# Sending the inner rows of eight shared tiles through DRAM, in one sequence with the experts' tiles

## The chip, the cores and the metric

The kernel runs on one core of a Trainium2 chip, as one program. The metric is the device time of one execution in microseconds (us). TensorE is called PE here, VectorE DVE, ScalarE ACT, GpSimd POOL and SyncE SP; each runs its own instructions strictly in order, and they wait for one another with semaphores. SP, ACT and POOL also issue DMAs, and a wait that stands ahead of a DMA in such a queue holds back all that stands behind it.

## The reference, cut to what matters

The first part (layer norm, attention over a context, gating) is not touched by the change. What follows it is a mixture of experts on 2048 tokens of 512 values, with 16 experts of inner width 352, four experts for each token, and two shared experts that every token passes:

```python
scores = jax.nn.softmax(xt @ Wg.T, axis=-1)
# two of four groups of experts are kept, and of these the best four experts: topi, weights
h = jax.nn.silu(jnp.einsum('td,eid->eti', xt, W1)) * jnp.einsum('td,eid->eti', xt, W3)
expert_out = jnp.einsum('eti,edi->etd', h, W2)
y = jnp.einsum('etd,te->td', expert_out, combine)
z = jax.nn.silu(xt @ Ws1.T) * (xt @ Ws3.T) @ Ws2.T
return (y + z).reshape(B, S, D)
```

The rows `h`, 352 values for each token, are called inner rows below: they are made by the two products with W1 and W3, and are the input of the product with W2.

## The kernel before

Tokens are worked in tiles of 128 rows. After attention there are three stages, in all 112 tiles: 16 tiles of the first shared expert (t = 0 to 15), 80 slots for the experts' tiles (E0 to E79 here; the last is never worked), and 16 tiles of the second shared expert. An expert's tile holds tokens of one expert, gathered by scattering each normed row four times into `xslot_d` in DRAM: POOL issues four indirect DMAs for each of the 16 token tiles (L626), out of a ring of four buffers `scat` that SP fills (L446).

Every fp32 operand of a product is split into a rounded part and a remainder (`xhi` and `xlo`, `hhi` and `hlo`, `whi` and `wlo`), and a product is three matmuls. So a tile goes through these steps:

- input rows: SP loads `xg` in four DMAs (L412), DVE transposes it into PSUM (L1492), ACT rounds it to `xhi` (L838), DVE takes the remainder `xlo` (L1499);
- `up` on PE: 24 matmuls of 352 columns (L1159 to L1161), twelve into a gate bank and twelve into bank 3;
- ACT takes silu of the gate bank into `sg` (L831), DVE multiplies with bank 3: the inner rows;
- the inner rows have to be turned, ACT rounds them to `hhi` (L877), DVE takes the remainder `hlo` (L1508);
- `down` on PE: nine matmuls of 512 columns (L1211 to L1213).

The stages differ in how inner rows are turned. In the first shared stage DVE writes `hx` (L1483), PE transposes it in three matmuls (L959, function `tr_h`), and the result is added to `x1` by DVE (L1561, called `res` in the rows). In the experts' stage DVE writes `hrow` (L1531), ACT stores it to `h_d` in DRAM in pieces of 96 values (L928, function `store_h`), SP loads it back as `hblk` (L468, `load_h`), and DVE turns 32x32 blocks (L1539, `h_turn`); there PE works the `up` of three later tiles between a tile's `up` and its `down`, which leaves the time for the way through DRAM, and the product is evacuated by ACT and stored.

While the first shared stage runs, ACT and DVE also split the second set of weights, in tiles 4 to 11 (L792 and L1448, two pieces for each tile), and DVE computes the routing tables in tiles 1 to 6.

The order of the instructions is set by two helpers. `pipeline` and `stream` write a stage as steps s; a part with a lead a works in step s on tile s + a, and the parts of a step stand in the order of the list. Before, the first shared stage is a `pipeline` on each engine, with the first experts' tiles added at its end by hand (`down_on`, `expert_high`, `expert_rows`, `first_row`), and the experts and the second shared stage are one `stream`. On PE a step of the first shared stage is `down` of tile s - 1, transposes of tile s, `up` of tile s + 1; a step of the experts is `down` of s - 2, `up` of s + 2. In the steps of SP, `load_scat` fetches the tile three ahead, and waits until the scatter of the tile before (s - 1) has left its buffer. Weights come in sets of 2.2 MB (`load_weights` and `next_raw` on POOL).

Of the kernel before, what the change touches and what calls it, by code (L numbers as in the profile page):

```python
# [14 lines left out]
P = 128  # L15
# [5 lines left out]
NQ = P // Q  # L21
# [24 lines left out]


# [48 lines left out]
def stream(eng, phases, ring, ramp=2):  # L96

    aheads = [a for ph in phases for a, fn in ph[2]]
    most, least = max(aheads), min(aheads)
    starts = [sum(ph[0] for ph in phases[:i]) for i in range(len(phases) + 1)]  # L100

    def peeled(s):
        for i in range(len(phases[0][2])):
            for p, (tiles, looped, parts, each_pass) in enumerate(phases):
                ahead, fn = parts[i]
                t = s + ahead - starts[p]
                if 0 <= t < tiles and fn:
                    fn(t, t % ring, t // ring)

    at = -max(0, most)  # L110
    for p, (tiles, looped, parts, each_pass) in enumerate(phases):
# [21 lines left out]
def xattn_moe(nc, x, heads, wg, wo, gn, wr, wexp, tables, qdecay, out):  # L133
    outer = ExitStack()
    with outer:
# [112 lines left out]
        sg = sb3("sg", [P, INTER], F32)  # L248
# [80 lines left out]
        def gate_bank(base, p):  # L329
            return 7 if base == NT and p else 2  # L330
# [19 lines left out]
        def _(sp):  # L350
# [82 lines left out]
            def store_y(t, r, turn):  # L433
                p = r % 2
                sp.wait_ge(y_out, 2 + NT + t + 1)
                sp.dma_start(rows(yslot_d, t), ysb[:, p, :]).then_inc(y_stored[p], 16)
# [6 lines left out]
            def load_scat(t, r, turn):  # L443
                if type(t) is not int or t >= XR:
# [16 lines left out]

            def load_h(t, r, turn):
                if type(t) is int and t == NR - 1:
                    return
                hold(sp, h_stored[r], 16 * (turn + 1))
                if type(t) is not int or t >= XG:
# [3 lines left out]
            sp.wait_ge(y_zeroed, 16 * (NR - NT * TOPK) // 8)  # L470
            stream(sp, [(NR, True, [(-1, load_h), (XG + 1, load_slots), (-3, store_y)], None),
                        (NT, False, [(0, None), (XG + 1, load_tile(NT + NR, xn_d)), (-4, store_out)], None)], XG)
# [191 lines left out]
        def _(act):  # L664
# [158 lines left out]
            def silu_g(base):  # L823
                def fn(t, p, half):
# [6 lines left out]
                    act.activation(sg[:, :], ps[:, gate_bank(base, p), 0:INTER], ACT.Silu).then_inc(silu, 1)  # L831
# [51 lines left out]
            def y_evac(t, p, half):  # L883
                act.wait_ge(mm2, NT + t + 1)
# [29 lines left out]
            def expert_high(t, p, half):  # L914
                if type(t) is int and t >= NT - 2:
                    x_high(NT)(t - NT + 2, p, 0)

            def x_high_e(t, p, half):
                if type(t) is not int or t >= 2:
                    x_high(NT)(t, p, half)  # L920

            def store_h(t, r, turn):
# [3 lines left out]
                if type(t) is not int or t >= XG:  # L926
                    hold(act, h_loaded[r], 16 * turn)
# [14 lines left out]
            pipeline(act, NT, [(1, x_high_on), (0, silu_on), (0, h_high(0)), (0, second_high), (0, exponents), (0, expert_high)], ramp=12)  # L942
            stream(act, [(NR, True, [(0, by_two(silu_g(NT))), (0, store_h), (-2, high_first), (2, by_two(x_high_e)), (-2, high_later), (-3, by_two(y_evac))], None),
                         (NT, True, [(0, by_two(silu_g(NT + NR))), (0, None), (-1, by_two(h_high(NT + NR))), (2, by_two(x_high(NT + NR))), (0, None), (0, None)], None)], XG)
# [3 lines left out]
        def _(pe):  # L948
# [184 lines left out]
            def up(base, which, halves=(0, 1)):  # L1133
                def fn(t, r, turn):
# [3 lines left out]
                    if base == NT:  # L1138
                        pe.wait_ge(silu, base + t - 1 if type(t) is not int or t else base)
# [94 lines left out]
            def routed(t, entry):  # L1234
                if type(t) is int:
# [15 lines left out]
            def down_on(t, r, turn):  # L1251
                if type(t) is int and t == NT - 1:
                    pe.wait_ge(rt_done, 1)
# [622 lines left out]
```

## Time and profile before

| what | us |
|---|---|
| median of 3 runs | 925.2 |
| lowest and highest run | 923.93 and 928.39 |
| profiled execution, its own time | 923.42 |
| span of the profiled execution | 921.8 |
| first shared stage, first `up` to the end of its last `down` | 235.8 to 350.5 |
| experts' stage after it, to the last `hblk` load | to 814.3 |

The profile is that of one execution. A row of the timeline gives the start in us from the start of the span, the duration, the engine, the line of kernel.py, the operation, and in brackets the idle time of the engine before it with what ended that. A row of windows gives the busy time of each engine in a stretch. The line of PE in 40 slices is nines almost throughout, and the granted clock (PEclk) is 9 in all of them.

### The profile page before, as it was taken

The numbers are of one execution on the slowest core, as the hardware profiler recorded it, in microseconds if no ns is written. First come the engines' busy times: TensorE is split into PE (matmuls) and PEld (weight loads), VectorE is DVE, ScalarE is ACT, GpSimd is POOL, SyncE is SP. The second block draws the span as 40 slices with busy tenths as digits, with TensorE's granted clock in tenths as the row PEclk, the third lists the DMA queues.
The fourth block names the chain that finished last, engine by engine and source line by source line (L and its number), as shares of the span: only waits on it lengthen the run. The fifth ranks groups of instructions, "written<-read, shape, count | busy, mean of one in ns | idle before, by whom it ended". The sixth has DMA issues, their size and how long they took to land.

```text
span 921.8 us, 19364 instructions
## 1 busy us (share of the span) xinstructions
PE 899.1 (98%) x4962; PEld 804.1 (87%) x4963; DVE 557.3 (60%) x1105; ACT 331.7 (36%) x708; POOL 494.5 (54%) x346
## 2 busy tenths in 40 slices
PE   8999998899989999999999999999999999999998
PEld 5778886688889999899999999999999999989997
DVE  6656676888896644544444444444444444459997
ACT  4556554354324322333333333333333333332221
POOL 1127777774167764435646664446666643136772
PEclk9999999999999999999999999999999999999999
DMA  6829996655578956778778777778777755588874
GB/s 216 267 100 393 384 404 232 225 187 175 189 232 296 306 208 206 230 204 253 238 240 246 251 247 202 239 244 259 249 251 250 245 173 158 163 228 248 274 247 145
DMA packets 180649, 218.97 MB, mean 238 GB/s; under 512 B 56576, under 2 KB 124160, under 8 KB 180224
## 3 DMA queue, kind: packets, MB, share of 16 engines
q1 hardware_dynamic: 118080, 123.49, 41.7%
q0 software_dynamic: 20816, 79.44, 25.9%
q10 hardware_dynamic: 41712, 15.54, 6.2%
q8 instruction: 20, 0.33, 0.2%
q14 instruction: 21, 0.17, 0.1%
HBM read 127.38 MB, written 91.03 MB: 237 GB/s over the span
## 4 chain that ended last, share of the span: by engine, by line
PE 78%; DVE 10%; issue 4%; ACT 3%; DMA 3%; ACTq 0%; DVEq 0%; POOL 0%; SPq 0%
PE ps L1159 15%; PE ps L1160 14%; PE ps L1161 14%; PE ps L1211 8%; PE ps L1213 8%; PE ps L1212 8%; PE ps L1012 2%; PE ps L1025 2%; DVE st L1456 1%; PE ps L959 1%; DVE res L1454 1%; DVE st L1273 1%; DMA hblk<-h_d 1%; ACT res L692 1%; PE ps L1045 1%
## 5 line engine op out<-in xcount | busy, mean ns | idle before, releaser
L1159 PE MATMUL ps<-whi,xhi 128*128 (+1 forms) x888 | 288.2, 325 | 1.6 <-issue 1.0
L1161 PE MATMUL ps<-whi,xlo 128*128 (+1 forms) x888 | 286.4, 323 | 0.0
L1160 PE MATMUL ps<-wlo,xhi 128*128 (+1 forms) x888 | 286.3, 322 | 0.0
L1531 DVE TENSOR_TENSOR hrow<-ps,sg 128x352 f32<-128x352 f32 x95 | 49.7, 524 | 214.4 <-ACT sg L831 211.1
L1159 PEld LDWEIGHTS ps<-whi,xhi 128*128 128x128 f32 x888 | 167.1, 188 | 6.5 <-issue 1.6
L1160 PEld LDWEIGHTS ps<-wlo,xhi 128*128 128x128 f32 x888 | 167.2, 188 | 3.9
L1161 PEld LDWEIGHTS ps<-whi,xlo 128*128 128x128 f32 x888 | 166.9, 188 | 0.0
L831 ACT ACTIVATE sg<-ps 128x352 f32<-128x352 f32 x111 | 51.5, 464 | 268.3 <-PE ps L1161 268.3
L838 ACT ACTIVATE xhi<-ps 128x512 fp32r<-128x512 f32 x112 | 66.9, 597 | 145.8 <-DVE ps L1492 145.8
L566 POOL TENSOR_TENSOR wlo<-raw,whi 128x2816 fp32r<-128x2816 f32 x16 | 100.7, 6293 | 2.4 <-POOL whi L564 0.2
L658 POOL DMA_INDIRECT raw<-yslot_d,sloti x64 | 68.1, 1064 | 57.7 <-DMA yslot_d<-ysb 22.6
L1499 DVE TENSOR_TENSOR xlo<-ps,xhi 128x512 fp32r<-128x512 f32 x112 | 76.9, 687 | 27.1 <-ACT xhi L838 26.8
L568 POOL CAST whi<-raw 128x1536 fp32r<-128x1536 f32 x16 | 23.5, 1468 | 126.2 <-PE ps L1213 126.2
L626 POOL DMA_INDIRECT xslot_d<-scat,sloti x64 | 62.8, 982 | 34.7 <-issue 17.7
L1492 DVE STREAM_TRANSPOSE ps<-xg 128x512 f32<-128x512 f32 x112 | 80.3, 717 | 0.0
L1211 PE MATMUL ps<-whi,hhi 128*128 (+1 forms) x168 | 67.3, 401 | 1.9 <-DVE hlo L1508 1.5
L1211 PE MATMUL ps<-whi,hhi_odd 128*128 (+1 forms) x165 | 65.2, 395 | 3.2 <-DVE hlo_odd L1508 3.2
L1213 PE MATMUL ps<-whi,hlo 128*128 (+1 forms) x168 | 66.6, 397 | 0.0
L1212 PE MATMUL ps<-wlo,hhi 128*128 (+1 forms) x168 | 66.2, 394 | 0.0
L1213 PE MATMUL ps<-whi,hlo_odd 128*128 (+1 forms) x165 | 65.0, 394 | 0.0
L1212 PE MATMUL ps<-wlo,hhi_odd 128*128 (+1 forms) x165 | 64.7, 392 | 0.0
L570 POOL TENSOR_TENSOR wlo<-raw,whi 128x1536 fp32r<-128x1536 f32 x16 | 56.3, 3518 | 2.3
(201 smaller groups left out, 1580.9 us busy)
## 6 DMA issues: line engine op xcount, KB each, us to landing
raw<-wexp_in POOLq DMA_DIRECT2D x18, 2176.0 KB, 11.4
xslot_d<-zero SPq DMA_DIRECT2D x10, 2048.0 KB, 21.7
xg<-xslot_d SPq DMA_DIRECT2D x320, 64.0 KB, 2.7
yslot_d<-ysb SPq DMA_DIRECT2D x80, 256.0 KB, 2.4
h_d<-hrow ACTq DMA_DIRECT2D x79, 192.0 KB, 2.9
hblk<-h_d SPq DMA_DIRECT2D x79, 192.0 KB, 2.6
xg<-xn_d SPq DMA_DIRECT2D x128, 64.0 KB, 3.6
xq<-x_in SPq DMA_DIRECT2D x16, 256.0 KB, 3.2
```

The source lines that it names most:

```text
L566: pool.tensor_tensor(wlo[:, p, up], raw[:, p, up], whi[:, p, up].bitcast(F32), ALU.subtract).then_inc(w13_ready, 1)
L626: pool.indirect_dma_start(out=xslot_d, out_offset=bass.IndirectOffsetOnAxis(ap=sloti[:, t * TOPK + k:t * TOPK + k + 1], axis=0), in_=scat[ ...
L658: pool.indirect_dma_start(out=gath[:, t % GR, k, :], out_offset=None, in_=yslot_d, in_offset=bass.IndirectOffsetOnAxis(ap=sloti[:, t * TOP ...
L838: act.activation(xhi[:, p, :], ps[:, p, :], ACT.Copy).then_inc(x_hi, 1)
L1159: pe.matmul(ps[:, bank, 0:INTER], xh, wh, start=(k == 0), stop=False)
L1160: pe.matmul(ps[:, bank, 0:INTER], xh, wl, start=False, stop=False)
L1161: mm = pe.matmul(ps[:, bank, 0:INTER], xl, wh, start=False, stop=(k == KT - 1))
L1211: pe.matmul(ps[:, 5 + p, :], hh, wh, start=(k == 0), stop=False)
L1212: pe.matmul(ps[:, 5 + p, :], hh, wl, start=False, stop=False)
L1213: mm = pe.matmul(ps[:, 5 + p, :], hl, wh, start=False, stop=(k == IC - 1))
L1492: dve.transpose(ps[:, p, :], xg[:, r, :].rearrange("p (c k j) -> p k c j", c=NQ, k=KT)).then_inc(x_tr, 1)
L1499: dve.tensor_tensor(xlo[:, p, :], ps[:, p, :], xhi[:, p, :].bitcast(F32), ALU.subtract).then_inc(x_lo, 1)
```

## The change

1. The first eight shared tiles stay as they were, but for one thing: DVE writes `hx` in an order that is already turned in blocks, since the shared expert's W2 rows are now stored in that order for all of its 16 tiles. That takes two instructions instead of one (`h_mult`).
2. The last eight shared tiles are now tiles -8 to -1 of the experts' sequence. Their inner rows go through DRAM like an expert's, they use gate banks 7 and 2 in turn instead of bank 2 alone, and PE transposes nothing for them. `add_later` adds their products to `x1`.
3. `stream` takes for each phase where it starts and its first tile, and all engines run one stream of three phases. In a step in which two phases meet, input rows' rounding (`x_high`) and remainder (`x_low`) stand ahead of the additions and of the inner rows' rounding and remainder.
4. On PE the last eight tiles are brought up two steps ahead: the order around the seam is up 7, up 8, down 6, transposes 7, up 9, down 7, up 10, up 11, down 8, up 12. The seam between shared tiles and experts, with its own hand-written order, is gone.
5. On SP the loads of inner rows stand in the same queue as the fetches for the scatter (`scat_later`, now four tiles ahead instead of three), and the first experts' rows are loaded at fixed steps (`load_rows`).

```diff
+HT = NT // 2
+HR = HT // XG
...
-            return 7 if base == NT and p else 2
+            return 7 if base == NT and p == 0 else 2
...
-            pipeline(sp, NT, [(XG, next_tile), (3, load_scat)], ring=XG)
-            sp.wait_ge(zeroed, 16 * (NR // 8))
-            sp.wait_ge(rt_done, 1)
...
+            def scat_later(t, r, turn):
+                if type(t) is int and t < 0:
+                    load_scat(t + NT, r, turn + NT // XG)
...
-            stream(sp, [(NR, True, [(-1, load_h), (XG + 1, load_slots), (-3, store_y)], None),
-                        (NT, False, [(0, None), (XG + 1, load_tile(NT + NR, xn_d)), (-4, store_out)], None)], XG)
+            stream(sp, [(0, 0, HT, False, [(0, None), (XG, next_tile), (0, None), (3, load_scat)], None),
+                        (NT, -HT, NR, True, [(-1, load_h), (XG + 1, load_rows), (-3, store_y), (XG, scat_later)], None),
+                        (NT + NR, 0, NT, False, [(0, None), (XG + 1, load_tile(NT + NR, xn_d)), (-4, store_out), (0, None)], None)], XG)
...
-            pipeline(pe, NT, [(-1, down_on), (0, tr_h(0)), (1, up_on)], ring=XG, ramp=3)
-            stream(pe, [(NR, True, [(0, None), (-2, down(NT, routed)), (2, up_e)], load_words),
+            stream(pe, [(0, 0, HT, False, [(-1, down(0, first)), (0, tr_h(0)), (1, up_on)], None),
+                        (NT, -HT, NR, True, [(0, None), (-2, down(NT, routed)), (2, up(NT, routed))], load_words),
...
-                    dve.tensor_tensor(hx[:, 0:INTER], ps[:, 3, 0:INTER], sg[:, :], ALU.mult).then_inc(h_ready, 1)
+                    up_half = ps[:, 3, 0:IC * P].rearrange("p (c k j) -> p c k j", c=NQ, k=IC)
+                    gates = sg[:, :].rearrange("p (c k j) -> p c k j", c=NQ, k=IC)
+                    turned = hx[:, :].rearrange("p (k c j) -> p c k j", k=IC, c=NQ)
+                    dve.tensor_tensor(turned[:, :, 0:2, :], up_half[:, :, 0:2, :], gates[:, :, 0:2, :], ALU.mult)
+                    dve.tensor_tensor(turned[:, 0:3, 2:3, :], up_half[:, 0:3, 2:3, :], gates[:, 0:3, 2:3, :], ALU.mult).then_inc(h_ready, 1)
...
+            stream(dve, [(0, 0, HT, False, [(2, x_turn_on), (1, x_low_on), (0, h_mult_on), (0, route_1), (0, route_2), (0, None), (-1, add_shared(0)),
+                                            (0, h_low_on), (0, second_set), (0, None)], None),
+                         (NT, -HT, NR, True, [(0, h_row(NT)), (-2, turn_first), (-2, low_first), (2, x_turn(NT)), (-2, turn_later), (2, x_low(NT)), (-2, low_later),
+                                              (-3, add_later), (0, second_later), (0, None)], None),
```

**On PE, where tiles 7 and 8 meet.** Before, `up` of a shared tile stands behind a `down` (here tile 7's, ending with L1213) and the three transposes of the next tile:

```order
L1213 MATMUL ps<-whi,hlo_odd 128x512
L1221 REGISTER_ALU
L959 MATMUL ps<-const,hx 128x128 [waits h_lo,h_ready]
L959 MATMUL ps<-const,hx 128x128 x2
L1137 REGISTER_ALU
L1159 MATMUL ps<-whi,xhi 128x352 [waits w13_ready,h_ready,x_lo]
```

In the changed kernel the last matmuls of tile 7's `up` are followed by the first of tile 8's:

```order
L1188 MATMUL ps<-wlo,xhi 128x352
L1189 MATMUL ps<-whi,xlo 128x352
L1187 MATMUL ps<-whi,xhi 128x352 [waits rt_done,w13_ready,silu,x_lo]
L1188 MATMUL ps<-wlo,xhi 128x352
L1189 MATMUL ps<-whi,xlo 128x352
```

No `down` and no transposes stand between the two, and tile 8's `up` waits for the routing tables (`rt_done`) and for an earlier silu.

**On DVE, tiles 7 and 8.** Before: input rows of the tiles ahead (L1492, L1499), the inner rows (`hx`), the addition of the tile before (`res`), the remainder `hlo`, two pieces of the second weights (`wlo`):

```order
L1492 STREAM_TRANSPOSE ps<-xg 128x512
L1499 TENSOR_TENSOR xlo<-ps,xhi 128x512
L1483 TENSOR_TENSOR hx<-ps,sg 128x352
L1561 TENSOR_TENSOR res<-res,ps 128x512
L1508 TENSOR_TENSOR hlo_odd<-ps,hhi_odd 128x384
L1448 TENSOR_TENSOR wlo<-raw,whi 128x272 x2
L1492 STREAM_TRANSPOSE ps<-xg 128x512
L1499 TENSOR_TENSOR xlo<-ps,xhi 128x512
L1483 TENSOR_TENSOR hx<-ps,sg 128x352
```

In the changed kernel, from the inner rows of tile 7 to those of tile 8 (`hrow`) and the next input rows:

```order
L1506 TENSOR_TENSOR hx<-ps,sg 128x4x2x32
L1507 TENSOR_TENSOR hx<-ps,sg 128x96
L1516 STREAM_TRANSPOSE ps<-xg 128x512
L1523 TENSOR_TENSOR xlo<-ps,xhi 128x512
L1585 TENSOR_TENSOR res<-res,ps 128x512
L1532 TENSOR_TENSOR hlo_odd<-ps,hhi_odd 128x384
L1468 TENSOR_TENSOR wlo<-raw,whi 128x272 x2
L1555 TENSOR_TENSOR hrow<-ps,sg 128x352
L1516 STREAM_TRANSPOSE ps<-xg 128x512
L1523 TENSOR_TENSOR xlo<-ps,xhi 128x512
```

The product is now two instructions, input rows moved behind it, and the inner rows of tile 8 stand behind the addition and the remainder that belong to tiles 6 and 7.

**On SP, at the end of the fetches for the scatter.** Before, the last fetch is followed by the first experts' rows (`xslot_d`), and the first load of inner rows comes only after six of these:

```order
L446 DMA scat<-xn_d 128x512 [waits scattered2]
L85 REGISTER_ALU
L85 COMPARE_AND_BRANCH
L446 DMA scat<-xn_d 128x512 [waits scattered3]
L454 TENSOR_LOAD order [waits y_zeroed,rt_done,zeroed]
L454 ISA x2
L412 DMA xg<-xslot_d 32x4x128 [waits scattered0,c_loaded,scattered1,scattered2,x_tr,scattered3]
L412 DMA xg<-xslot_d 32x4x128 x3
```

In the changed kernel, from the load of input rows of tile 13 to the load of inner rows of tile 9:

```order
L415 DMA xg<-xn_d 32x4x128 [waits x_tr]
L415 DMA xg<-xn_d 32x4x128 x3
L453 DMA scat<-xn_d 128x512 [waits scattered0]
L493 DMA hblk<-h_d 128x384 [waits h_stored0,c_loaded]
L415 DMA xg<-xn_d 32x4x128 [waits x_tr]
L415 DMA xg<-xn_d 32x4x128 x3
L453 DMA scat<-xn_d 128x512 [waits scattered1]
L493 DMA hblk<-h_d 128x384 [waits h_stored1,c_loaded]
```

A load of inner rows stands behind each fetch that waits for a scatter.

## Rows read from the trace of the kernel before

**Rows 1.** The page, busy us, share of the span, instructions:

```profile
PE 899.1 (98%) x4962; PEld 804.1 (87%) x4963; DVE 557.3 (60%) x1105; ACT 331.7 (36%) x708; POOL 494.5 (54%) x346
```

**Rows 2.** Timeline of PE, shared tiles (first two), then experts' (others); start, duration:

```profile
300.44 0.49 PE L959 MATMUL ps<-const,hx 128*128 128x128 f32 x3
306.70 0.49 PE L959 MATMUL ps<-const,hx 128*128 128x128 f32 x3
...
561.39 0.32 PE L1159 MATMUL ps<-whi,xhi 128*128 x1
567.32 0.32 PE L1159 MATMUL ps<-whi,xhi 128*128 x1
```

**Rows 3.** Timeline of PE around the `up` of shared tile 7:

```profile
288.20 0.41 PE L1159 MATMUL ps<-whi,xhi 128*128 128x352 f32 x1
...
292.12 0.39 PE L1211 MATMUL ps<-whi,hhi 128*128 128x512 f32 x1
...
294.20 0.49 PE L959 MATMUL ps<-const,hx 128*128 128x128 f32 x3
294.45 0.41 PE L1159 MATMUL ps<-whi,xhi 128*128 128x352 f32 x1
```

**Rows 4.** Timeline of DVE after the transposes of tile 8:

```profile
301.49 0.56 DVE L1508 TENSOR_TENSOR hlo<-ps,hhi 128x384 fp32r<-128x384 f32 x1 [0.17 <-ACT hhi L877]
301.96 0.78 DVE L1448 TENSOR_TENSOR wlo<-raw,whi 128x272 fp32r<-128x272 f32 x2
302.67 0.72 DVE L1492 STREAM_TRANSPOSE ps<-xg 128x512 f32<-128x512 f32 x1
```

**Rows 5.** SP's queue: two fetches for the scatter, then waits from 256 to 345 us:

```profile
307.17 0.35 SPq L446 DMA_DIRECT2D scat<-xn_d  x1
...
312.29 0.35 SPq L446 DMA_DIRECT2D scat<-xn_d  x1
...
SPq L446 <- DMA xslot_d<-scat,sloti: 42.9, 12, 15.8
```

**Rows 6.** DMAs to landing: L928, L468; then `xg` at 270:330 and 420:600:

```profile
DMA to landing us min/median/max: 2.1/2.9/11.4
...
DMA to landing us min/median/max: 2.1/2.6/9.9
...
xg<-xn_d SPq DMA_DIRECT2D x36, 64.0 KB, 3.5
...
xg<-xslot_d SPq DMA_DIRECT2D x125, 64.0 KB, 2.4
```

**Rows 7.** Timeline at the first experts' tiles: POOL's weight load, DVE, PE:

```profile
356.39 0.96 POOL L480 DMA_DIRECT2D raw<-wexp_in  x1
...
367.09 0.59 DVE L1539 STREAM_TRANSPOSE ps<-hblk 128x384 f32<-128x384 f32 x1 [3.31 <-DMA hblk<-h_d]
...
369.01 0.50 PE L1211 MATMUL ps<-whi,hhi_odd 128*128 x1 [0.83 <-DVE hlo_odd L1508]
```

**Rows 8.** Timeline of PE, tiles 1 and 3, then of DVE in tiles 0 and 1:

```profile
258.82 0.50 PE L1211 MATMUL ps<-whi,hhi_odd 128*128 128x512 f32 x1 [0.88 <-DVE hlo_odd L1508]
...
273.04 0.50 PE L1211 MATMUL ps<-whi,hhi_odd 128*128 128x512 f32 x1 [1.46 <-DVE hlo_odd L1508]
...
243.21 0.29 DVE L1586 TENSOR_TENSOR gcmp<-gcmp,const 128x128 f32<-128x128 f32 x1
...
251.55 0.53 DVE L1483 TENSOR_TENSOR hx<-ps,sg 128x352 f32<-128x352 f32 x1 [1.02 <-ACT sg L831]
252.00 0.16 DVE L1613 COPY ntile<-ps 128x16 f32<-128x16 f32 x1
252.19 0.43 DVE L1614 TENSOR_TENSOR tcmp<-ntile,const 128x256 f32<-128x256 f32 x1
```

**Rows 9.** Windows: busy us of PE, PEld, DVE, ACT, POOL; clock, DMA share, GB/s:

```profile
306.00:312.00 6.00, 6.00 (x36) 5.61 (x35) 3.60 (x7) 2.08 (x5) 4.47 (x6) 1.00 0.92 310
312.00:318.00 6.00, 6.00 (x36) 5.63 (x35) 3.44 (x8) 2.08 (x5) 4.53 (x5) 1.00 0.97 328
390.00:410.00 20.00, 19.77 (x112) 18.35 (x112) 9.73 (x17) 6.88 (x14) 7.13 (x3) 1.00 0.74 224
```

**Rows 10.** DMA queue of the stores of inner rows, 420 to 600 us: packets, MB, share:

```profile
q10 hardware_dynamic: 16374, 6.10, 12.5%
```

**Rows 11.** POOL's last scatter; the scatters' issues at 270:330 with us to landing:

```profile
340.14 0.97 POOL L626 DMA_INDIRECT xslot_d<-scat,sloti  x1 [0.30 <-issue]
...
xslot_d<-scat,sloti POOLq DMA_INDIRECT x47, 4.0
```

More of the change, by code:

```diff
@@ L96, in stream @@
 def stream(eng, phases, ring, ramp=2):
-    aheads = [a for ph in phases for a, fn in ph[2]]
+    aheads = [a for ph in phases for a, fn in ph[4]]
     most, least = max(aheads), min(aheads)
-    starts = [sum(ph[0] for ph in phases[:i]) for i in range(len(phases) + 1)]
+    starts = [ph[0] for ph in phases] + [phases[-1][0] + phases[-1][2]]
     def peeled(s):
-        for i in range(len(phases[0][2])):
-            for p, (tiles, looped, parts, each_pass) in enumerate(phases):
+        for i in range(len(phases[0][4])):
+            for p, (start, first, tiles, looped, parts, each_pass) in enumerate(phases):
                 ahead, fn = parts[i]
-                t = s + ahead - starts[p]
-                if 0 <= t < tiles and fn:
+                t = s + ahead - start
+                if first <= t < tiles and fn:
                     fn(t, t % ring, t // ring)
     at = -max(0, most)
-    for p, (tiles, looped, parts, each_pass) in enumerate(phases):
+    for p, (start, first, tiles, looped, parts, each_pass) in enumerate(phases):
         lo = starts[p] + min(max(0, ramp - least), tiles)
@@ L460, in load_slots, with load_rows @@
                 load_tile(NT, xslot_d)(t, r, turn)
+            def load_rows(t, r, turn):
+                if type(t) is not int or t > 5:
+                    load_slots(t, r, turn)
+                elif t < 0:
+                    load_tile(0, xn_d)(t + NT, r, turn)
+                elif t == 0:
+                    sp.wait_ge(zeroed, 16 * (NR // 8))
+                    sp.wait_ge(rt_done, 1)
+                    load_slots(0, 0, 0)
+                elif t == 1:
+                    load_slots(1, 1, 0)
+                elif t == 4:
+                    load_slots(2, 2, 0)
+                    load_slots(3, 3, 0)
+                elif t == 5:
+                    load_slots(4, 0, 1)
+                    load_slots(5, 1, 1)
+            def scat_later(t, r, turn):
+                if type(t) is int and t < 0:
+                    load_scat(t + NT, r, turn + NT // XG)
             def load_h(t, r, turn):
@@ L912, in exponents, with second_later @@
                     act.activation(top8f[:, :, 0:TOPK], top8f[:, :, 0:TOPK], ACT.Exp).then_inc(rt_exp, 1)
[L914 to L920, printed above, removed]
+            def second_later(t, p, half):
+                if type(t) is int and t < 0:
+                    second_high(t + NT, p, half)
             def store_h(t, r, turn):
@@ L1138, in fn @@
                     if base == NT:
-                        pe.wait_ge(silu, base + t - 1 if type(t) is not int or t else base)
+                        pe.wait_ge(silu, base + t - 1)
+                        if type(t) is int and t == -HT:
+                            pe.wait_ge(rt_done, 1)
                     elif 1 in halves:
@@ L1234, in routed @@
             def routed(t, entry):
+                if type(t) is int and t < 0:
+                    return 0, 1
                 if type(t) is int:
```

83 lines of the change are left out of this document (34 added, 49 removed).

## The prediction

> **What bounds the kernel now.** I read the page first: PE is busy for 98% of the span [rows 1]. So only two things can move the time by much: less work on PE, or a new stall of PE. Then the timeline of PE, a shared tile against an expert's. From transposes to transposes a shared tile takes 306.70 - 300.44 = 6.26 us, an expert's tile from `up` to `up` 567.32 - 561.39 = 5.93 us [rows 2]. The pieces: `up` with its slow first matmul 292.12 - 288.20 = 3.92 us, `down` 294.20 - 292.12 = 2.08 us, transposes 0.25 us [rows 3]; an expert's `up` is then 5.93 - 2.08 = 3.85 us. The difference of 0.33 us is what a PE transpose of inner rows costs a tile. Last, the stalls: PE waits for DVE by 0.88 us in tile 1 and 1.46 us in tile 3, where the routing tables delay `hlo` [rows 8], and by 0.83 us at the second expert's tile, whose inner rows came late from DRAM behind a weight load [rows 7].
>
> **The change part by part.** (a) Eight tiles lose their transposes: 8 x 0.33 = 2.64 us less on PE, which nothing else can hide. The granted clock is full at every stretch I looked at (1.00 in [rows 9]), so no gain or loss comes from there.
>
> (b) The old seam to the experts goes. It cost PE 0.83 us: the load of the second tile's rows sat in flight while 2.2 MB of weights, issued at 356.39, were moving [rows 7]. In the new order the experts come in mid-stream, with three `up`s between a tile's `up` and its `down`. The weights still come, some 5 us later, since POOL splits the shared W2 only after tile 15's `down`, which is now behind two experts' `up`s. What such a load costs mid-stream is read from a 20 us window around one: PE busy 19.77 us, 0.23 us lost [rows 9]. I take 0.83 - 0.23 = 0.60 us gained, between 0 and 0.83.
>
> (c) `h_mult` is two instructions. One of 352 columns lasts 0.53 us and the next starts 0.45 us after it; 256 columns start the next 0.46 us later, with 0.43 us of their own; 128 columns last 0.29 us [rows 8]. Two pieces of 256 and 96 so cost between 0.1 and 0.3 us more; I take 0.13, since issue overlaps the tail of an instruction by some 0.08 us. It matters only where DVE is late already: tiles 0, 1 and 3 with the routing tables, and tile 6, four times: 0.5 us, from 0.4 to 1.2. In the other tiles the product ends about 0.85 us before PE reaches the transposes.
> The Trainium skill (VectorE: DVE Perf Modes, The TRN2 errata) gives an fp32 `tensor_tensor` (N + 151)/0.96 ns, so a second instruction would add 0.16 us; by that the term would be 0.63 us, an estimate. The trace agrees for 256 columns (0.43 us [rows 8], 0.42 by the page).
>
> (d) The new seam. I go along PE from the old clock, where tile 7's `up` ends at 292.12 [rows 3]. Up 8 to 295.97 (3.85 us), down 6 to 298.05, transposes to 298.30, the gate half of up 9 (half of 3.92 us) to 300.2. Its second half overwrites bank 3 and waits for the row product of tile 8. On DVE that product now stands behind the addition of tile 6, which waits for down 6; behind `hlo` of tile 7, which in the old rows starts 1.05 us after the transposes do (301.49 - 300.44) [rows 2, 4]; and behind two pieces of weights, 0.71 us (302.67 - 301.96) [rows 4]. So: 298.05 + 1.05 = 299.1, + 0.47 + 0.71 = 300.3, + 0.53 for the product: 300.8. PE waits 0.6 us, between 0 (if the pieces overlap better) and 0.9 (two more signals).
>
> (e) Inner rows of tile 8. Their store is issued at 301.3. SP loads them only behind the fetch for the scatter in its queue, which in the old trace comes free at 307.17 [rows 5]; POOL sets this pace and nothing of POOL changes. Load issued at 307.6. A landing takes 2.6 us in the median, but here the DMA engines are 92 to 97% taken [rows 9], and `xg` loads take 3.5 us where they take 2.4 among the experts [rows 6]: 2.6 x 3.5/2.4 = 3.8 us, 311.4. From the turn on DVE to the first matmul of `down` are 369.01 - 367.09 = 1.92 us [rows 7]: 313.3. PE wants it after up 9 (302.8), down 7, up 10 and up 11: 302.8 + 2.08 + 2 x 3.85 = 312.6. It waits 0.7 us. Bounds: with the fastest landing of a load, 2.1 us, 0; with the slowest, 9.9 us [rows 6], 6.8. I take 0.7, by the `xg` loads of the same stretch.
> Tile 9: load at 312.29 + 0.4, ready at 312.7 + 3.8 + 1.92 = 318.4; PE wants it at 313.3 + 2.08 + 3.85 = 319.2. Each later tile gains 5.93 - 5.12 = 0.8 us on the fetches (312.29 - 307.17 [rows 5]). Nothing more is lost there.
>
> (f) First experts' rows. The last scatter is issued at 340.14 and lands by 340.14 + 0.97 + 4.0 = 345.1 [rows 11]. SP then issues four loads, about 2 us, landing in 2.4, and transpose, rounding and remainder take 2 us: E2 is ready at 351.4. PE, at 319.2 + 4 x 5.93 = 342.9 after E0's `up`, comes to E2's after down 13, up E1, down 14: 342.9 + 2 x 2.08 + 3.85 = 350.9. 0.5 us late; 0 if POOL, which waited for PE before its last two tiles, ends sooner.
>
> SP's other waits, POOL's indirect DMAs and ACT's extra stores cost nothing themselves: ACT is busy 2.08 of 6 us there, DVE 3.6 of 6 [rows 9], and DVE gets about 0.5 us of turning more for each tile.
>
> The sum: -2.64 - 0.60 + 0.5 + 0.6 + 0.7 + 0.5 = -0.94 us. The profiled execution took 923.42 us, so 922.5 for one like it; it lies 1.8 us under the median of the three runs, 925.2, and I take the same difference there: 924.3 us. A change of 0.5% is 4.6 us, about what a measurement of this kernel can tell from no change.
>
> **The rivals.** *All covers hold.* DVE's order costs nothing at up 9, the load of tile 8 lands in 2.1 us, the scatter ends in time: -2.64 - 0.83 + 0.4 = -3.1, or 922.1 us. For it speaks the 60% of DVE [rows 1]; against it that SP cannot issue tile 8's load before 307.6.
>
> *The DMA engines are over-full: slower.* The stretch of scatters is at 92 to 97% [rows 9]. A store of inner rows takes 12.5% x 180 us / 30 = 0.75 us of all engines [rows 10], in the 180 us and 30 stores of that window, and the load back about as much again: of 5.93 us, 25%. If shares add, demand is 1.19 of what there is, and the scatters of a tile take 6.1 us instead of 5.12. Over eight tiles that is 7.8 us, less some 1.7 us that POOL waited for PE at the end: about 6 us, and E2's rows are that much later, one for one. That gives -0.94 + 6 = +5.1: 930.3 us. It turns the change into a loss from 0.9 us of slip, and into one over 0.5% from 5.5 us. Against it: `xg` loads in this stretch still land in 3.5 us [rows 6], which engines at their limit would not give, and the share is busy time of packets, not of bandwidth (328 GB/s there [rows 9]).
> The Trainium skill (DMA: Bandwidth & Descriptors, Specifications) wants at least 512 B for each transfer, below which an engine reads, modifies and writes; it speaks against this change, whose stores go in pieces of 96 values. The trace agrees that these stores are dear: 6.10 MB in 16374 packets take 12.5% [rows 10]. By that rule alone it is this rival, and 930.3 us.
>
> *The transposes were hidden.* PE's records are modelled at their ends, and if the 0.33 us were waiting for the product and not work, taking the transposes away gives nothing: 925.2 - 0.94 + 2.64 = 926.9. Against it: 0.25 us pass between the start of the transposes and the next `up`, with no wait shown [rows 3].
>
> **How the numbers follow.** Forecast (a sum near -0.9, from -2.5 to +2): 0.60, at 924.3. All covers hold: 0.20. Over-full engines: 0.13. Hidden transposes: 0.05. Anything else 0.02. The range runs from 921.5 (all covers, and a little of the runs' own spread) to 930.5 (the over-full engines at their price); beyond it are the higher half of that rival, and half of the rest. Faster by over 0.5% needs a gain of 4.6 us, more than (a) and (b) hold: 0.03. Slower by over 0.5%: 0.10. Within: 0.87.
>
> **What would show it.** In the changed kernel's trace: no PE transposes after tile 7, and 5.93 us for each shared tile from tile 12 on; PE waits of 0.6 us in the second half of tile 9's `up`, 0.7 us at tile 8's `down`, 0.5 us at E2's `up`, none at the second expert's `down`; SP's fetches for the scatter still 5.1 us apart. Wrong: fetches 6 us apart, PE waiting for `hblk` in more than one tile, or PE's waits in tiles 1 and 3 longer by more than 0.3 us each.

## The result and the profile after

The changed kernel takes 928.44 us (median of 20 runs, 925.34 to 930.73), the kernel before 923.82 us (median of 20 runs, 921.52 to 928.39). The ratio is 1.0047, its 95% interval 1.0036 to 1.0057: slower, by 4.6 us. The forecast was no change that can be measured, at 924.3 us; the time lies inside the range given, and on the other side of no change from the sum, which was a gain of 0.94 us. The profiled execution took 928.44 us, its span is 926.8 us.

On the page of the changed kernel PE is about as full as before [rows 1] (97% of the span, 98% before), with fewer instructions and more busy time:

```profile
PE 903.5 (97%) x4938; PEld 806.3 (87%) x4939; DVE 561.9 (61%) x1121; ACT 333.1 (36%) x708; POOL 493.8 (53%) x346
```

So matmuls became longer or further apart somewhere. To find where, I compared the two timelines of PE at points with equal work behind them: the first matmul of the second product (`down`) of every 128-row tile, counted in the order of work (the sixteen shared tiles, then E0, E1 and so on).

| stretch, first matmul of a `down` to first matmul of a later one | before | after | difference |
|---|---|---|---|
| shared tile 0 to expert tile E2 (the seam lies in it) | 124.91 | 125.97 | +1.06 |
| E2 to E8 | 36.07 | 36.62 | +0.55 |
| E8 to E74 (66 tiles, no stall in either trace) | 390.06 | 392.92 | +2.86 |
| E74 to tile 13 of the second shared stage | 110.08 | 110.47 | +0.39 |
| sum | 661.12 | 665.98 | +4.86 |

The first stretch has the seam that the prediction spoke of; the third, the largest difference, has nothing that it spoke of. The third is also the firmest: as shown below, kernels with the same buffer layout repeat its time to the hundredth, while the first stretch takes 123.5 to 125.5 us in twelve single executions that work it with the instructions of before.

**The seam.** The timeline of PE in the changed kernel, the rows with a wait and one of the matmuls that follow the longest (start, duration, then the wait in brackets):

```profile
301.09 0.43 PE L1187 MATMUL ps<-whi,xhi 128*128 128x352 f32 x1 [0.39 <-DVE hrow L1555]
...
315.52 0.50 PE L1239 MATMUL ps<-whi,hhi 128*128 128x512 f32 x1 [2.15 <-DVE hlo L1532]
...
316.94 0.63 PE L1240 MATMUL ps<-wlo,hhi 128*128 128x512 f32 x1
...
319.07 0.50 PE L1187 MATMUL ps<-whi,xhi 128*128 128x352 f32 x1
...
401.19 0.49 PE L1239 MATMUL ps<-whi,hhi 128*128 x1 [0.63 <-DVE hlo L1532]
```

Tile 9's `up` waits 0.39 us for the row product, tile 8's `down` 2.15 us for its remainder. That `down` then takes 319.07 - 315.52 = 3.55 us where one took 2.08 [rows 3]: its matmuls last 0.63 us instead of 0.39. The windows of the changed kernel say why (busy us of PE, PEld, DVE, ACT, POOL; clock, DMA share, GB/s):

```profile
310.00:330.00 20.00, 17.85 (x93) 16.22 (x92) 11.61 (x22) 5.82 (x13) 15.37 (x16) 0.91 1.02 347
...
316.20:319.00 2.80, 2.80 (x8) 2.19 (x7) 2.24 (x5) 1.52 (x4) 2.19 (x3) 0.50 1.05 385
```

The granted clock is 0.50 from 316.2 to 319.0, the lower of the two levels (1.2 GHz); where the same stretch had been at 1.00 before [rows 9]. The chain back from the wait is on DVE and in SP's queue:

```profile
313.76 0.59 DVE L1563 STREAM_TRANSPOSE ps<-hblk 128x384 f32<-128x384 f32 x1 [3.24 <-DMA hblk<-h_d]
```

```profile
301.91 0.34 SPq L453 DMA_DIRECT2D scat<-xn_d  x1
302.30 4.33 SPq L415 DMA_DIRECT2D xg<-xn_d  x4
309.04 0.34 SPq L453 DMA_DIRECT2D scat<-xn_d  x1
309.47 0.38 SPq L493 DMA_DIRECT2D hblk<-h_d  x1
```

The load of tile 8's inner rows (L493) goes out at 309.47, right behind a fetch for the scatter that waited for its buffer until 309.04, and lands 4.3 us later.

**The experts.** An even step runs from the first matmul of an even tile's `down` (input `hhi`) to that of the next tile's (`hhi_odd`), an odd step from there to the next `hhi`. The timeline of PE in the changed kernel, first matmuls of three successive `down`s, and in each of the two `up`s between them three matmuls of its second half:

```profile
562.08 0.39 PE L1239 MATMUL ps<-whi,hhi_odd 128*128 x1
...
566.72 0.32 PE L1188 MATMUL ps<-wlo,xhi 128*128 x1
566.88 0.32 PE L1189 MATMUL ps<-whi,xlo 128*128 x1
567.04 0.32 PE L1187 MATMUL ps<-whi,xhi 128*128 x1
...
567.99 0.39 PE L1239 MATMUL ps<-whi,hhi 128*128 x1
...
572.49 0.33 PE L1187 MATMUL ps<-whi,xhi 128*128 x1
572.66 0.33 PE L1188 MATMUL ps<-wlo,xhi 128*128 x1
572.82 0.33 PE L1189 MATMUL ps<-whi,xlo 128*128 x1
...
573.98 0.39 PE L1239 MATMUL ps<-whi,hhi_odd 128*128 x1
```

From `hhi_odd` to `hhi` a step takes 5.91 us, from `hhi` to `hhi_odd` 5.99 us. The difference is in the second half of the `up` of even tiles, where matmuls start 0.166 us apart and not 0.16. No wait is shown and the clock is 1.00. An even step of the kernel before, with three matmuls of the same place:

```profile
565.23 0.39 PE L1211 MATMUL ps<-whi,hhi 128*128 x1
...
569.73 0.32 PE L1159 MATMUL ps<-whi,xhi 128*128 x1
569.89 0.32 PE L1160 MATMUL ps<-wlo,xhi 128*128 x1
570.04 0.32 PE L1161 MATMUL ps<-whi,xlo 128*128 x1
...
571.15 0.39 PE L1211 MATMUL ps<-whi,hhi_odd 128*128 x1
```

It takes 5.92 us, with these starts 0.15 to 0.16 us apart. Over E8 to E74 the even steps average 6.00 us and the odd ones 5.91; before, 5.92 and 5.90. 33 pairs of tiles times 11.907 - 11.820 are the 2.86 us of the table.

### The profile page after: what moved, and what is told of

The parts are those of the page before. It is cut to its first block, busy times and chain, and to the rows that moved or that the text cites. A ratio compares the mean times of both kernels' runs of the same rounds, so it can differ in the third digit from the quotient of the medians.

```text
span 926.8 us, 19226 instructions
## 1 busy us (share of the span) xinstructions
PE 903.5 (97%) x4938; PEld 806.3 (87%) x4939; DVE 561.9 (61%) x1121; ACT 333.1 (36%) x708; POOL 493.8 (53%) x346
## 4 chain that ended last, share of the span: by engine, by line
PE 74%; DVE 8%; issue 7%; DMA 5%; ACT 3%; POOL 3%; ACTq 0%; DVEq 0%; SPq 0%; POOLq 0%
PE ps L1187 14%; PE ps L1189 13%; PE ps L1188 13%; PE ps L1239 8%; PE ps L1241 8%; PE ps L1240 7%; POOL xslot_d L651 3%; DMA xslot_d<-scat,sloti 2%; PE ps L1038 2%; PE ps L1051 2%; DMA h_d<-hrow 1%; DVE st L1476 1%; DVE res L1474 1%; DVE st L1293 1%; ACT res L717 1%
## 5 line engine op out<-in xcount | busy, mean ns | idle before, releaser
L1555 DVE TENSOR_TENSOR hrow<-ps,sg 128x352 f32<-128x352 f32 x103 | 53.9, 523 | 223.3 <-ACT sg L856 219.4
```

## Experiments

Steps named even and odd below are means over these 33 pairs. Single executions of these kernels differ by up to 4 us in stretches that an edit doesn't touch, so where only one execution was made, the verdict rests on the steps and not on the time. The ratios are those on record; they differ a little from the quotients of the two medians (1.0005 and 1.0016 for e3), which all lie inside the intervals given.

**What slows the even tiles.** Two lines of the change could reach into the experts' loop, whose instructions are otherwise the same: the order of the gate banks, and the size of the buffer `sg`, which the diff ahead of the prediction leaves out (`sb3("sg", [P, INTER], F32)` became `[P, IC * P]`, for the view in `h_mult`). Each was put into the kernel before, alone; neither adds an instruction, so the place where the loop's instructions lie, a third possible cause, stays as it was.

```diff
-            return 7 if base == NT and p else 2
+            return 7 if base == NT and p == 0 else 2
```

> The kernel before with one line changed: among the experts the first product of the even tiles goes to PSUM bank 7 and that of the odd ones to bank 2, as in the changed kernel (before: odd to 7, even to 2). In the changed kernel an even tile's step takes 6.00 us and an odd one's 5.91; before 5.92 and 5.90. Theory A, the bank order makes the even tiles' second half slow: steps 6.00 and 5.91 here too, 33 pairs times 0.085, +2.9 us, about 926.7. Theory B, the addresses in SBUF that move with the larger gate buffer, and theory C, where the loop's instructions lie: 5.92 and 5.90, no change beyond 0.5 us.

e1: 924.57 us against 924.73, ratio 0.9993 (0.9970 to 1.0015); steps 5.92 and 5.90. The banks do nothing.

```diff
-        sg = sb3("sg", [P, INTER], F32)
+        sg = sb3("sg", [P, IC * P], F32)
...
-                    act.activation(sg[:, :], ps[:, gate_bank(base, p), 0:INTER], ACT.Silu).then_inc(silu, 1)
+                    act.activation(sg[:, 0:INTER], ps[:, gate_bank(base, p), 0:INTER], ACT.Silu).then_inc(silu, 1)
...
```

(The two products of DVE read `sg[:, 0:INTER]` in the same way.)

> The kernel before with the gate buffer as large as the changed kernel has it (384 instead of 352 numbers a row, so that everything allocated behind it lies 128 bytes further on; nothing else is changed). Theory B (addresses): even steps 6.00, odd 5.91, about +2.9 us. Theories A (banks) and C (place of the instructions): 5.92 and 5.90, within 0.5 us of before.

e2: 928.89 us against 924.73, ratio 1.0037 (1.0013 to 1.0061). The timeline of PE, first matmuls of two successive `down`s:

```profile
566.59 0.39 PE L1211 MATMUL ps<-whi,hhi 128*128 x1
...
572.58 0.39 PE L1211 MATMUL ps<-whi,hhi_odd 128*128 x1
```

5.99 us, as in the changed kernel; E8 to E74 takes 392.92 us, to the hundredth what it takes there. A buffer that is 128 bytes longer, and whose extra bytes nothing here reads, makes the kernel before slower by 0.4%. The reverse in the changed kernel, first by the banks alone (shared tile 7 goes to bank 7, so that tile 8 finds bank 2 free), then by the addresses alone (the longer buffer is laid over the small table behind it):

```diff
-            return 7 if base == NT and p == 0 else 2
+            return 7 if base == NT and p or base == 0 and type(t) is int and t == HT - 1 else 2
...
```

> The changed kernel with the bank order of before among the experts (odd tiles to bank 7, even to bank 2; tile 7 of the shared expert goes to bank 7 so that tile 8 finds bank 2 free). Theory A: all steps 5.90 to 5.92 and 2.9 us less, about 925.5. Theories B and C: even steps stay at 6.00 and the time within 0.5 us of 928.4. The wait of 2.15 us at tile 8 stays in all.

e4: 928.87 us, ratio to before 1.0032 (1.0015 to 1.0050); steps 6.00 and 5.91.

```diff
-        sg = sb3("sg", [P, IC * P], F32)
-        ntile = sb3("ntile", [P, 2, E], F32)
+        sgn = sb3("sgn", [P, INTER + 2 * E], F32)
+        sg, ntile = sgn[:, 0:IC * P], sgn[:, INTER:INTER + 2 * E].rearrange("p (a e) -> p a e", a=2)
```

> The changed kernel with the gate buffer at its larger size laid over the small table that follows it, whose numbers are not read through it, so that every other buffer has the address it has in the kernel before; nothing else is changed. Theory (addresses): even steps among the experts back from 6.00 to 5.91 us, 2.9 us less, about 925.6. Rival, the larger gate buffer itself and not what it moves: even steps stay at 6.00, within 0.5 us of the changed kernel. The wait of 2.15 us at tile 8's second product stays in both.

e5: 924.64 us, ratio to before 1.0003 (0.9987 to 1.0020), and the steps are back:

```profile
566.40 0.39 PE L1239 MATMUL ps<-whi,hhi 128*128 x1
...
572.32 0.39 PE L1239 MATMUL ps<-whi,hhi_odd 128*128 x1
```

5.92 us, 390.06 us from E8 to E74. So addresses alone turn this change from the same into slower.

**Which buffer.** The kernel before again, with 128 unused bytes a row put ahead of one buffer, so that all behind it move. One execution each.

```diff
+        sb3("pad", [P, IC * P - INTER], F32)
         hrow = sb3("hrow", [P, 2, IC * P], F32)
```

> The kernel before with 128 unused bytes a row ahead of the inner rows' buffer hrow, so that only hrow and hblk move. If one of the two sets the even tiles' pace: even steps 6.00, odd 5.91. If it is hhi_odd and hlo_odd, or one of the buffers ahead of them (tables, ysb, scat): 5.92 and 5.90.

e7: 5.92 and 5.90 (928.16 us; the time went elsewhere, 3.9 us of it at the start of the second shared stage).

```diff
+        sb3("pad", [P, IC * P - INTER], F32)
         hhi.append(sb3("hhi_odd", [P, IC * P], F32R))
```

> The kernel before with 128 unused bytes a row ahead of hhi_odd, so that hhi_odd, hlo_odd (the weights that TensorE loads for the odd tiles' second product), hrow and hblk move. If these weights' addresses set the pace: even steps 6.00 and odd 5.91 here and 5.92 and 5.90 with the pad ahead of hrow. If it is ysb, scat or the tables: 5.92 and 5.90 in both.

e8: 6.00 and 5.91 (926.74 us). So it is `hhi_odd` and `hlo_odd`, the rows that TensorE loads as weights for the odd tiles' `down`. The same pad between the two, then pads of twice and three times the size ahead of both:

> The kernel before with the 128 unused bytes between hhi_odd and hlo_odd, so that hlo_odd moves and hhi_odd stays (hrow and hblk move too; the pad ahead of hrow showed that they do nothing). If the slow second halves of the even tiles' up come from hlo_odd: even steps 6.00 as with the pad ahead of hhi_odd. If from hhi_odd: 5.92. If each has its share: between, near 5.96.

e9: 5.92 and 5.94 (927.62 us). The even steps stay, as if `hhi_odd` set them; but the odd tiles' `down` itself, which reads these rows, takes 2.10 us instead of 2.06, which none of the three theories had. (In the changed kernel it takes 2.09, and the `up` behind it gives 0.02 back.)

> The kernel before with 256 unused bytes ahead of hhi_odd instead of 128. If it is the place within 256 bytes that counts (before 160, in the changed kernel 32): 160 again, even steps 5.92. If any move of the two buffers away from where they lay does it: 6.00.

> The kernel before with 384 unused bytes ahead of hhi_odd. If the place within 256 bytes counts, it is 32 as in the changed kernel: even steps 6.00. If only the changed kernel's own addresses are slow: 5.92.

e10, with 256 bytes: 5.92 and 5.90 (922.18 us). e11, with 384 bytes: 6.00 and 5.91 (924.95 us). Timeline of PE, even steps of the first, then of the second:

```profile
564.29 0.39 PE L1212 MATMUL ps<-whi,hhi 128*128 x1
...
570.21 0.39 PE L1212 MATMUL ps<-whi,hhi_odd 128*128 x1
```

```profile
565.31 0.39 PE L1212 MATMUL ps<-whi,hhi 128*128 x1
...
571.31 0.39 PE L1212 MATMUL ps<-whi,hhi_odd 128*128 x1
```

Moves by 0 and 256 bytes give 5.92, by 128 and 384 bytes 6.00: in these four, what counts is the place within 256 bytes, not where the buffers lie. Four more layouts asked for the rule: `hhi_odd` alone moved; `hhi` and `hlo` alone; both pairs by the same 128 bytes; the odd pair by 64.

> The kernel before with 128 unused bytes ahead of hhi_odd and 128 ahead of hlo_odd: hhi_odd lies at 32 within 256 bytes as in the changed kernel, hlo_odd, hrow and hblk at 160 as before. If hhi_odd alone sets the slow second halves: even steps 6.00. If it takes both: 5.92, perhaps with a longer odd step as in the run in which hlo_odd alone had moved (5.94).

> The kernel before with 128 unused bytes ahead of hhi and 128 behind the gate buffer: hhi and hlo (the even tiles' pair) lie at 224 within 256 bytes instead of 96, and everything behind the gate buffer lies at 256 more, the same place within 256. If the rule holds for every such pair: the odd tiles' up, which stands ahead of the product with hhi, takes some 0.08 us more or less, odd steps near 5.98 or 5.82. If it is one of the odd pair alone: 5.92 and 5.90 as before.

> The kernel before with 128 unused bytes ahead of hhi, so that hhi, hlo, the gate buffer and all behind it lie 128 further on: within 256 bytes hhi 224, hhi_odd 32, both at places that were slow when one pair alone had moved, but their distance is 64 as before. If the distance counts: even steps 5.92. If either place counts: 6.00.

> The kernel before with 64 unused bytes ahead of hhi_odd: the distance of the pairs is 128 within 256 bytes instead of 64. No theory gives a number for this distance: 5.92 if only 192 is slow, 6.00 or between if 64 is the one good distance seen so far.

e13 to e16, one execution each, took 928.73, 927.76, 928.46 and 927.55 us. All layouts side by side. The places are counted from the buffers' sizes in the order in which they are allocated; the traces hold no addresses, so what is certain is how far each buffer moved against before. The last column is the 33 pairs of E8 to E74 against before:

| runs | place of `hhi`, `hlo` within 256 B | of `hhi_odd`, `hlo_odd` | even step | odd step | us more |
|---|---|---|---|---|---|
| before, banks (e1), addresses back (e5), `hrow` (e7), 256 B (e10), two instructions (e12) | 96, 96 | 160, 160 | 5.92 | 5.90 | 0 |
| after, longer `sg` (e2), later fetch (e3), banks back (e4), 128 B (e8), 384 B (e11) | 96, 96 | 32, 32 | 6.00 | 5.91 | 2.86 |
| `hhi_odd` alone (e13) | 96, 96 | 32, 160 | 6.00 | 5.90 | 2.42 |
| `hlo_odd` alone (e9) | 96, 96 | 160, 32 | 5.92 | 5.94 | 1.32 |
| even pair moved (e14) | 224, 224 | 160, 160 | 5.98 | 5.91 | 2.20 |
| both moved by 128 B (e15) | 224, 224 | 32, 32 | 5.98 | 5.91 | 2.20 |
| odd pair by 64 B (e16) | 96, 96 | 224, 224 | 5.92 | 5.96 | 2.20 |

In the slow rows one second half of the two in a pair of tiles takes 1.98 us instead of 1.90 (in none of the first row, and none of e9's): that of the even tiles' `up`, but in the last row that of the odd tiles'. With `hhi` and `hlo` where they were, the place of `hhi_odd` goes with it. But moving the even pair does it too, in the same place of the step, and the distance between the pairs is not it either: 64 bytes in the first row and in the sixth, and the sixth is slow. (With the even pair the gate buffer moved as well, and in the sixth layout all that lies behind it; these were not moved alone.) A rule is not found. What is shown is that the layout of before is the best of seven, and that the pace follows the layout: the kernels of the first row take 390.06 us from E8 to E74, each of them, and those of the second 392.92 (e6 below, with the layout of the first row, 390.14). Why matmuls that read neither buffer start later stays open.

**The seam.** Is the load of tile 8's inner rows late because of its place in SP's queue, or because the DMA engines are full? The fetch was put one step later, so that the load stands behind one that has waited for less:

```diff
-                        (NT, -HT, NR, True, [(-1, load_h), (XG + 1, load_rows), (-3, store_y), (XG, scat_later)], None),
+                        (NT, -HT, NR, True, [(-1, load_h), (XG + 1, load_rows), (-3, store_y), (3, scat_later)], None),
```

> The changed kernel, but from tile 8 on the fetch for the scatter stands 3 tiles ahead on SP instead of 4, so that the load of tile 8's inner rows stands behind a fetch that waited for less. Theory: the 2.15 us wait at tile 8's second product comes from that queue order, and the 1.4 us of half clock behind it from the wait; both go, 3.5 us less, about 924.9 (span 923.3), clock 1.00 in 310 to 330. Rival, the load is late because the DMA engines are full (share 1.02 there): the wait stays within 0.5 us of 2.15 and the time within 1 us of 928.4. The even steps stay at 6.00.

e3: 926.24 us, ratio to before 1.0005 (0.9980 to 1.0029), 2.6 us less than the kernel with the banks put back, which has the wait and ran on the same chip. The wait at tile 8 is gone, and the even steps stay at 6.00. SP's queue, windows (columns as above) and PE in this kernel:

```profile
303.96 0.34 SPq L453 DMA_DIRECT2D scat<-xn_d  x1
306.34 0.34 SPq L493 DMA_DIRECT2D hblk<-h_d  x1
```

```profile
310.00:330.00 20.00, 19.42 (x109) 17.84 (x109) 13.07 (x26) 7.01 (x17) 15.42 (x16) 1.00 1.03 341
```

```profile
321.67 0.50 PE L1239 MATMUL ps<-whi,hhi_odd 128*128 128x512 f32 x1 [0.58 <-DVE hlo_odd L1532]
```

The engines are as full (1.03), so their share alone does not make the wait; with the other order, counted from tile 0's `down` in each trace, the load goes out 4.9 us earlier. What is left is 0.58 us at tile 9. The clock stays at 1.00. That the wait alone does not settle the clock is shown by the kernel with the banks put back: it waited 2.27 us at the same place and ran on at full clock, so the seam cost it 1.4 us less (124.59 us from tile 0 to E2, where the changed kernel took 125.97). PE and windows of that kernel:

```profile
316.00 0.50 PE L1239 MATMUL ps<-whi,hhi 128*128 128x512 f32 x1 [2.27 <-DVE hlo L1532]
316.34 0.39 PE L1240 MATMUL ps<-wlo,hhi 128*128 128x512 f32 x1
```

```profile
316.10:318.00 1.90, 1.90 (x9) 1.52 (x10) 1.23 (x3) 1.38 (x4) 1.29 (x3) 1.00 0.96 351
```

And by the kernel with the addresses put back, whose wait of 2.17 us was again followed by half clock:

```profile
316.60:319.90 3.30, 3.30 (x8) 2.62 (x9) 2.32 (x5) 1.59 (x4) 2.43 (x3) 0.50 1.04 384
```

Of three profiled executions with this wait, two lost the clock behind it. The Trainium skill (TensorE: Matmul & The Clock Gate, Part 1: The HAM clock gate) says that an idle engine falls to 1.2 GHz and gets 2.4 GHz back when it is busy; these two executions agree, with 0.50; the third, with the same wait, kept 1.00, and no run here shows what told them apart. Nor does the length of a wait tell it elsewhere: behind one of 1.89 us (E2, at 376.43) e16 was at 0.50, behind one of 3.38 us (at 849.49) e7 stayed at 1.00.

**Both.** The two edits that gave something, together:

> The changed kernel with both edits, the addresses of before and the fetch for the scatter 3 tiles ahead. If the two costs are separate: 2.5 us (what the later fetch gave) and 2.9 us less than the changed kernel, 923.0, some 1 to 2 us below the kernel before on the same chip. Rival, they overlap (one of them hides the other): 925 or more.

e6: 922.19 us against 924.28, ratio 0.9972 (0.9956 to 0.9988): 2.4 us less than with the addresses alone, and below both kernels. The two costs are separate. From tile 0 to E2 it takes 121.77 us, 3.14 less than before (whose own stretch is good to about 1 us, as said); 0.93 of that is given back by E8, where a store of inner rows issued at 380.00, beside a weight load issued at 379.21, lands 12.7 us later. Windows, then PE:

```profile
310.00:330.00 20.00, 20.00 (x115) 18.84 (x114) 13.23 (x25) 6.19 (x15) 15.16 (x16) 1.00 1.01 345
```

```profile
397.63 0.50 PE L1239 MATMUL ps<-whi,hhi 128*128 x1 [0.97 <-DVE hlo L1532]
```

**The product in two instructions.** The kernel before with this alone, at its own addresses (left out of the cut: the three views as in the change, the gate buffer laid over the small table as in e5, and the shared expert's W2 rows in the turned order):

```diff
-                    dve.tensor_tensor(hx[:, 0:INTER], ps[:, 3, 0:INTER], sg[:, :], ALU.mult).then_inc(h_ready, 1)
+                    dve.tensor_tensor(turned[:, :, 0:2, :], up_half[:, :, 0:2, :], gates[:, :, 0:2, :], ALU.mult)
+                    dve.tensor_tensor(turned[:, 0:3, 2:3, :], up_half[:, 0:3, 2:3, :], gates[:, 0:3, 2:3, :], ALU.mult).then_inc(h_ready, 1)
...
```

> The kernel before with the shared tiles' product written in two instructions in the turned order (and the rows of the shared expert's second weights in that order), at the addresses of before; all sixteen tiles still go through the transposes. The prediction had 0.13 us for each of the four tiles whose second product waits, 0.5 us in all. By the changed kernel's trace it is 0.20 us up to tile 5. Here: 0.2 us up to tile 5 and none from tile 8 on, if the waits are those of tiles 1 and 3 alone; 0.13 for each tile, 2 us by tile 15, if the product is on every tile's path.

e12: 924.55 us in one execution. Against before, the `down`s of tiles 1, 3 and 6 each start 0.06 to 0.07 us later, 0.20 in all by tile 7, and nothing is added up to tile 14. On DVE, in the changed kernel:

```profile
251.53 0.42 DVE L1506 TENSOR_TENSOR hx<-ps,sg 128x256 f32<-128x256 f32 x1 [1.02 <-ACT sg L856]
251.87 0.25 DVE L1507 TENSOR_TENSOR hx<-ps,sg 128x96 f32<-128x96 f32 x1
252.03 0.16 DVE L1637 COPY ntile<-ps 128x16 f32<-128x16 f32 x1
```

The next instruction starts 0.50 us after the product, where it was 0.45 [rows 8].

## Why the prediction was wrong, step by step

**(a) The transposes, -2.64 us: right in size.** At the addresses of before (e5) the shared tiles from 9 on take 5.90 and 5.92 us (forecast 5.93). The rival that they were hidden is out. In the changed kernel itself the slow even steps take back some 0.30 us of it by E2 (tile 9 to E2 takes 53.49 us, 53.19 in e5).

**"The granted clock is full at every stretch I looked at (1.00 in [rows 9]), so no gain or loss comes from there": failed.** The rows were right for a PE that never stops. Behind a wait of 2.15 us the clock was at 0.50, and `down` 8 took 1.5 us more. A wait that the change adds must be priced with what the clock does after it.

**(b) The old seam, -0.60 us: more, by the wrong subtraction.** The stall of 0.83 us is gone, and with it a second one at the next expert's tile that the rows ahead of the prediction leave out (375.50 below). The weight load that stood behind them goes out at 366.21 in the changed kernel, in mid-stream, and PE has no wait from 315.52 to 401.19. So it costs nothing there. The 0.23 us that I took for it belongs to the next set of weights (399.63 below), which both kernels load: issued at 382.25 before and at 383.32 now, where it shows as the 0.63 us at 401.19. In e4 and e5 PE doesn't wait there. PE in the kernel before:

```profile
375.50 0.49 PE L1211 MATMUL ps<-whi,hhi 128*128 x1 [0.23 <-issue]
...
399.63 0.50 PE L1211 MATMUL ps<-whi,hhi 128*128 x1 [0.23 <-issue]
```

What the old seam costs also differs by execution: in thirteen executions that have it, from E0 to E2 takes 12.4 to 14.0 us (13.47 in the trace before), so 0.83 is one value of several.

**(c) The product in two instructions, +0.5 us: too high.** 0.20 us, shown by itself in one execution (0.1 to 0.3 in the five with the change, by tile 5). The second instruction starts under the tail of the first: 0.05 us from start to start, not 0.13, and three tiles instead of four.

**(d) Tile 9's second half, +0.6 us: right mechanism,** 0.39 us.

**(e) Tile 8's inner rows, +0.7 us: right mechanism, wrong size.** 2.15 us, and 1.5 us of half clock behind it. The failed sub-step is "POOL sets this pace and nothing of POOL changes": the fetch came free at 309.04 and not at 307.17 [rows 5]. The same 1.9 us, counted from tile 0's `down`, are in the two other executions with this queue order. POOL did keep its pace; the landing of its scatter did not. The last indirect DMA of the scatter that this fetch waited for, before and in the changed kernel (its row on POOL, then the row of DMAs issued in that instant, with us to landing):

```profile
302.75 0.97 POOL L626 DMA_INDIRECT xslot_d<-scat,sloti  x1 [0.30 <-issue]
...
xslot_d<-scat,sloti POOLq DMA_INDIRECT x1, 4.4
```

```profile
302.67 0.97 POOL L651 DMA_INDIRECT xslot_d<-scat,sloti  x1 [0.30 <-issue]
...
xslot_d<-scat,sloti POOLq DMA_INDIRECT x1, 6.3
```

With the banks put back it takes 6.4 us too, with the later fetch (e3, e6) 4.8. So slower landings, as the rival of the over-full engines has them, have a part in this wait beside the order. The first store of inner rows, issued at 301.13, and a fetch issued at 301.91 that takes 5.4 us to land (3.2 before) are in flight with it; which of them slows it was not tried. The landing of the load itself took 4.3 us for 3.8. I had kept 6.8 as the upper bound and put no chance on what lies between.

**(f) E2's rows, +0.5 us: nothing.** No wait there. The sum was wrong too: a landing is counted from the start of the issue, so the 0.97 us stand in it twice (and its terms add up to 351.5, not 351.4). Counted once, the rows are ready at 350.5, ahead of PE's 350.9.

**The over-full engines: half of a rival.** DMAs in the changed kernel, 270 to 330 us, with us to landing in the last column, have the fetches at 4.1, the inner rows at 4.9:

```profile
scat<-xn_d SPq DMA_DIRECT2D x11, 256.0 KB, 4.1
...
hblk<-h_d SPq DMA_DIRECT2D x5, 192.0 KB, 4.9
xslot_d<-scat,sloti POOLq DMA_INDIRECT x47, 4.2
```

The engines' share is 1.02 from 310 to 330 us (0.88 before), and the fetches are 5.7 us apart from 296.42 to 324.85, not 5.1. One scatter that landed 1.9 us later made most of the wait under (e). But in the median the scatters land in 4.2 us (4.0 before [rows 11]), and no expert's rows were late. Its time, 930.3, was nearer than the forecast, for another reason; that 928.44 lies inside the range is luck, since this rival alone had set the upper end.

**What was not in the sum: the addresses, +2.9 us.** This is the step whose absence decided the sign: with the addresses put back and the late load still there, the change measures 1.0003 (0.9987 to 1.0020). The parts were priced from the instructions that the change adds and removes. A line that changes only a buffer's size has none, and was not among them.

With what was measured, from tile 0 to E2: -2.64 + 0.30 - 0.83 - 0.23 + 0.20 + 0.39 + 2.15 + 1.5 = +0.84, where the traces differ by 1.06; the rest is less than single executions differ by. Then 2.86 for the pairs of E8 to E74, and 0.9 in the two short stretches around them, 0.4 of it again even steps and 0.4 the longer wait at 401.19, whose cause I did not test. Without the two unforeseen costs the kernel is near the one of "all covers hold", whose time was given as 922.1; it measured 922.19. That the two agree to 0.1 us is luck: the gain was given as 3.1 us from 925.2, the median of three runs, and is 2.1 us from 924.28, and the wait of (d) is still in it.

## What to carry to other kernels

When a change makes a buffer longer, list what lies behind it and keep the addresses, or measure the size alone: 128 bytes cost more here than eight tiles' transposes gave. Look at a trace for work whose instructions have not changed and compare its pace to the hundredth of a microsecond; a difference there points away from the part that was edited. And in a queue that waits in order, ask of each moved transfer which wait now stands ahead of it: putting one fetch one step later gave 2.4 to 2.6 us.

## What the hardware showed that was not expected

Matmuls of 352 columns start 0.160 or 0.166 us apart, by the place within 256 bytes of buffers that they do not read, at a granted clock of 1.00 and with ACT and DVE idle (neither has a row between 571.97 and the `down` at 573.98 shown above). The Trainium skill (SBUF — State Buffer, Operand start alignment) asks that an operand starts at a multiple of its element's size. All seven layouts meet that, and differ by up to 0.087 us for two tiles.

The clock also fell where PE had hardly waited. In the changed kernel's profile PE had been busy 3.82 of 4 us, for the most part with transposes and matmuls of 16 columns, and then:

```profile
236.00:240.00 4.00, 3.82 (x33) 3.70 (x31) 3.86 (x23) 3.68 (x10) 1.18 (x2) 1.00 0.31 118
...
241.00:244.50 3.50, 3.50 (x13) 3.24 (x12) 3.26 (x17) 0.18 (x1) 1.61 (x2) 0.51 0.58 162
```

Six of the eighteen profiled executions, of kernels with and without the change, have such a stretch, which begins between 240 and 245 us; what sets it off was not tried.
